# Attention's scores from three rounded products, expert weights split where they are used, a shorter choice of tokens

## The reference, cut to what matters

```python
h = ln(x) * g + b + shift(t)
q, k, v = split(h @ Wqkv.T)                 # 16 heads of 64
q, k = ln64(q), ln64(k)                     # per head, with scale and bias
o = softmax(q @ k.T / 8) @ v                # 256 x 256 scores per head and batch
x = x + o @ Wout.T
gate = softmax(x @ Wgate.T)                 # 8 experts
vals, idx = top_k(gate.T, 512)              # each expert takes its 512 best tokens
y = gelu(ln(x[idx]) @ fc1[e].T + b1) @ fc2[e].T + b2
x[idx] += y * vals
```

## Time and profile before

| | |
|---|---|
| median of three runs | 1504.6 us (1504.4 to 1504.73) |
| profiled execution, its own time | 1506.99 us |
| its span, first to last instruction | 1505.2 us |
| granted TensorE clock over the span | 0.98 |
| TensorE (PE) busy | 1411.1 us, 94% |
| ScalarE (ACT) busy | 974.7 us, 65% |
| VectorE (DVE) busy | 959.1 us, 64% |
| GpSimd (POOL) busy | 777.3 us, 52% |
| DMA | 138.79 MB, 92 GB/s |

### The profile page before, as it was taken

The page is one execution under the profiler, slowest core; times in us unless marked ns, Lnnn a source line. Parts: engine busy times, 40 slices in busy tenths (PEclk is TensorE's granted clock), DMA queues, the critical chain, the costliest instruction groups (busy, mean ns, idle before and its releaser), DMA issues. The chain is left out here.

```text
span 1505.2 us, 31379 instructions
## 1 busy us (share of the span) xinstructions
PE 1411.1 (94%) x9953; PEld 1164.0 (77%) x9953; DVE 959.1 (64%) x2244; ACT 974.7 (65%) x2601; POOL 777.3 (52%) x736
## 2 busy tenths in 40 slices
PE   4799999997999999999999999999999787999997
PEld 3799999985667777777777777777777566899996
DVE  5876666644576676676667667667756558565652
ACT  4556666545788788787787878878877640345452
POOL 3566667544455554654655554565555420264633
PEclk9899999998999999999999999999999999899998
DMA  5342222110122221221222221222222335267652
GB/s 154 91 135 68 65 68 70 47 36 21 50 71 78 85 79 64 91 84 64 76 84 82 79 84 63 77 91 85 69 66 78 101 107 229 83 194 228 196 168 28
DMA packets 92391, 138.79 MB, mean 92 GB/s; under 512 B 8656, under 2 KB 61824, under 8 KB 92160
## 3 DMA queue, kind: packets, MB, share of 16 engines
q1 hardware_dynamic: 84032, 126.30, 25.8%
q0 software_dynamic: 6144, 8.39, 2.9%
q10 hardware_dynamic: 2112, 2.88, 0.6%
HBM read 87.20 MB, written 50.35 MB: 91 GB/s over the span
## 5 line engine op out<-in xcount | busy, mean ns | idle before, releaser
L1301 POOL TENSOR_TENSOR prob<-prob,share_p 128x512 f32<-128x512 f32 x256 | 274.1, 1076 | 373.7 <-DVE share_p L1407 373.7
L1401 DVE TENSOR_REDUCE shift<-bank 128x2 f32<-128x512 f32 x256 | 164.8, 685 | 245.1 <-PE bank L1060 245.0
L1199 ACT ACTIVATE prob<-bank,shift 128x256 f32<-128x256 f32 x512 | 235.5, 473 | 99.6 <-DVE shift L1401 99.6
L147 PE MATMUL bank<-wqkv_h,rowsT_h 128*128 128x512 f32 x384 | 160.0, 417 | 5.7 <-PEq L313 3.5
L1086 PE MATMUL bank<-pT,v 128*64 128x256 f32 x1024 | 140.5, 396 | 16.4 <-ACT pT L1273 16.3
L147 PE MATMUL bank<-wqkv_l,rowsT_h 128*128 128x512 f32 x384 | 152.4, 397 | 0.0
L147 PE MATMUL bank<-wqkv_h,rowsT_l 128*128 128x512 f32 x384 | 152.4, 397 | 0.0
L1060 PE MATMUL bank<-landing 64*128 64x256 f32 x1024 | 145.4, 402 | 2.7 <-ACT prob L1199 2.7
L1073 PEld LDWEIGHTS bank<-ident,prob 128*128 128x128 f32 x1024 | 109.3, 141 | 43.9 <-issue 41.8
L1296 POOL TENSOR_TENSOR raw_qk<-raw_qk,rq 128x512 f32<-128x512 f32 x128 | 138.0, 1094 | 8.4 <-DVE rq L1355 8.4
L1073 PE MATMUL bank<-ident,prob 128*128 128x128 f32 x1024 | 140.5, 280 | 0.6 <-POOL prob L1301 0.4
(11 more groups left out here) (285 smaller groups left out, 4062.3 us busy)
## 6 DMA issues: line engine op xcount, KB each, us to landing
ew_raw<-in_fc1s SPq DMA_DIRECT2D x32, 256.0 KB, 3.2
split_w1h<-ew_h SPq DMA_DIRECT2D x32, 256.0 KB, 2.0
split_w1l<-ew_l SPq DMA_DIRECT2D x32, 256.0 KB, 2.5
ew_raw<-in_fc2s SPq DMA_DIRECT2D x32, 256.0 KB, 2.9
split_w2h<-ew_h SPq DMA_DIRECT2D x32, 256.0 KB, 2.1
split_w2l<-ew_l SPq DMA_DIRECT2D x32, 256.0 KB, 2.5
ew_h<-split_w1h SPq DMA_DIRECT2D x8, 1024.0 KB
ew_l<-split_w1l SPq DMA_DIRECT2D x8, 1024.0 KB
```

Source lines behind the costliest of these rows:

```text
L147: last = nc.tensor.matmul(out, a, b, start=(n == 0), stop=(n == 3 * len(ks) - 1))
L1199: last = nc.scalar.activation(prob[at][:, n, :], score_bank[side][:, n * T:(n + 1) * T], ACT.Exp, bias=shift[:, at, n:n + 1], scale=-1.0, ...
L1301: nc.gpsimd.tensor_tensor(prob[at][:, :, :], prob[at][:, :, :], share[:, at, :].unsqueeze(2).to_broadcast([P, TT, T]), ALU.mult).then_inc( ...
L1401: nc.vector.tensor_reduce(shift[:, s % 2 * 2 + side, :], score_bank[side][:, :].rearrange("p (n m) -> p n m", n=TT), AX, ALU.min).then_inc ...
```

## The change

Five things are changed together.

1. **Scores.** The normalised q and k, after transposing, scale and bias, go back to `raw`; ScalarE rounds each 128 x 512 block into `qT_h`/`kT_h` (pairs `HIGH_PAIR`) and GpSimd subtracts into `qT_l`/`kT_l` (`LOW_PLACE`). `scores` makes three fp32r products a side in place of one fp32 product. The first scores of a batch wait for six low parts, the fifth pair's for all eight.
2. **The order of a batch.** The `h` fill goes from slot 8 to 2, the second `proj` from slot 10 to 6, the q and k fills to slots 5 and 7 to 13; the value chunks from pairs 3 and 4 to 4 and 5; the normalising of q and k starts one slot earlier; GpSimd's residual sum goes from pair 6 to 5, and `a_l` and the low parts come behind both scalings of a pair.
3. **Expert weights.** Only experts 0 and 1 are split during attention, one piece a batch instead of four. For experts 2 to 7 the raw weights (2 MB an expert) are loaded in the experts' stage; ScalarE makes the high parts, VectorE the low parts of `fc1`'s weights, and GpSimd, behind its scatters, those of `fc2`'s.
4. **The choice of tokens.** The threshold is spread by one transpose, the masks are compared in place from the gates, and the counts go through fp32r products directly; the waits for the stores move from the end of attention into the choice's SyncE program.
5. **Records** are fp32 and not fp32r, and their 32 products go in turn to four column groups of the array.

```diff
-TR_FILLS = [("x2", 0, 1), ("gates", 0, 3), ("proj", 0, 4), ("qk", 0, 5), ("qk", 1, 6), ("qk", 2, 7), ("h", 0, 8), ("qk", 3, 9),
-            ("proj", 1, 10), ("qk", 4, 11), ("qk", 5, 12), ("qk", 6, 13), ("qk", 7, 14)]
+TR_FILLS = [("x2", 0, 1), ("h", 0, 2), ("gates", 0, 3), ("proj", 0, 4), ("qk", 0, 5), ("proj", 1, 6)] + [("qk", j, 6 + j) for j in range(1, 8)]
...
+QK_ORDER = [1, 0, 2, 3, 4, 6, 5, 7]
+HIGH_PAIR = [3, 4, 5, 5, 6, 6, 7, 7]
+LOW_PLACE = [(3,1),(4,1),(5,1),(5,1),(6,1),(6,1),(7,1),(7,1)]
...
-CHUNK_PAIRS = [6, 6, 7, 7, 0, 0, 1, 1, 3, 3, 4, 4]
+CHUNK_PAIRS = [6, 6, 7, 7, 0, 0, 1, 1, 4, 4, 5, 5]
...
-MEAN_SLOT, SEED_PAIR, NORM_SLOT = (1, 5), (1, 3), (4, 8)
+MEAN_SLOT, SEED_PAIR, NORM_SLOT = (1, 5), (1, 3), (3, 7)
...
-X2_PAIR = 6
+PIECE_PAIRS = 2, 3
+X2_PAIR = 5
...
+        raw = landing[:, 0:2, :].rearrange("p i (m n) -> p (i m) n", n=512)
...
+        qT_h, qT_l, kT_h, kT_l = (sbuf(s, n, [P, 12, T], F32R) for n in ("qT_h", "qT_l", "kT_h", "kT_l"))
+        v = [landing[:, 2 + i, :].rearrange("p (t n) -> p t n", t=TT) for i in range(2)]
...
+        o_h, o_l = (sbuf(s, f"o_{p}", [P, HW // P + 2, T], F32R) for p in "hl")
...
+        def block_of(parts, j, its):
+            e = QK_ORDER[j]
+            part = parts[e % QKC // 2]
+            at = 4 + 4 * its if e % 2 else 0
+            return part[:, at:at + 4, e // QKC * P:(e // QKC + 1) * P]
...
+                def store_piece(b, odd):
+                    wait(sp, ew_piece, 32, b, 32)
+                    for n, part in enumerate((ew_h, ew_l)):
+                        sp.dma_start(piece(halves[odd * 2 + n], b, odd), part[:, :].bitcast(F32)).then_inc(ew_stored, 16)
...
                     b = t + 3
                     if live(b):
                         wait(sp, tr_h, 1, b - 1, 1)
                         sp.dma_start(x1[:, :, :], x1_rows[bass.ds(b * T, T), :].rearrange("(t p) d -> p t d", p=P)).then_inc(x1_in, 16)
-                    pieces(t, (2,))
+                    if live(t):
+                        store_piece(t, odd)
+                    if live(t) and live(t + 1):
+                        load_piece(t + 1, 1 - odd)
...
-                sp.wait_ge(x2_stored, 16 * NB)
-                sp.wait_ge(x2n_stored, 16 * NB)
-                sp.wait_ge(ew_stored, 128 * NB)
...
                     if s == 0:
-                        wait(pe, out_qk, 8, t, 8)
+                        wait(pe, qk_lo, 8, t, 6)
+                    if s == 4:
+                        wait(pe, qk_lo, 8, t, 8)
                     wait(pe, exped, H, t, 2 * s)
+                    at = s if s < 4 else s + 4 * odd
                     for n in range(TT):
-                        for side in range(2):
-                            r = slice(side * HD, (side + 1) * HD)
-                            mm = nc.tensor.matmul(score_bank[side][:, n * T:(n + 1) * T], qT[odd][r, s, n * P:(n + 1) * P],
-                                                  kT[odd][r, s, :], start=True, stop=True)
-                            if n == TT - 1:
-                                mm.then_inc(scored, 1)
+                        for i, (q, k) in enumerate(((qT_h, kT_h), (qT_h, kT_l), (qT_l, kT_h))):
+                            for side in range(2):
+                                r = slice(side * HD, (side + 1) * HD)
+                                mm = nc.tensor.matmul(score_bank[side][:, n * T:(n + 1) * T], q[r, at, n * P:(n + 1) * P],
+                                                      k[r, at, :], start=(i == 0), stop=(i == 2))
+                                if n == TT - 1 and i == 2:
+                                    mm.then_inc(scored, 1)
...
                         wait(act, tr_qk, 8, b, j + 1)
-                        if isinstance(b, int) and b == 1:
-                            act.wait_ge(wo_lo, FIRST_LO + 1)
-                        dst, g = (qT, QN_G) if j % 4 < 2 else (kT, KN_G)
-                        nc.scalar.activation(dst[its][:, j % 2 * 4:j % 2 * 4 + 4, j // 4 * P:(j // 4 + 1) * P],
-                                             tr[:, :].rearrange("p (m n) -> p m n", m=4), ACT.Identity,
+                        g = QN_G if QK_ORDER[j] % QKC < 2 else KN_G
+                        nc.scalar.activation(raw_block(j), tr[:, :].rearrange("p (m n) -> p m n", m=4), ACT.Identity,
                                              bias=cols[:, g + 1:g + 2], scale=cols[:, g:g + 1]).then_inc(out_qk, 1)
...
-                        wait(act, tr_qk, 8, b - 1, e + 1)
+                        wait(act, qk_lo, 8, b - 1, QK_ORDER.index(e) + 1)
...
+                        for j in range(8):
+                            if live(t + 1) and HIGH_PAIR[j] == s:
+                                wait(act, out_qk, 8, t + 1, j + 1)
+                                nc.scalar.activation(block_of((qT_h, kT_h), j, 1 - odd), raw_block(j), ACT.Copy).then_inc(qk_hi, 1)
...
-                        if live(t) and s % 2 == 0:
-                            wait(act, ew_in, 64, t, 16 * (s // 2 + 1))
-                            wait(act, ew_stored, 128, t, 32 * (s // 2))
-                            nc.scalar.activation(ew_h[:, :], ew_raw[:, :], ACT.Copy).then_inc(ew_hi, 1)
+                        if live(t) and s == PIECE_PAIRS[0]:
+                            wait(act, ew_piece, 32, t, 16)
+                            wait(act, ew_stored, 32, t - 1, 32)
+                            nc.scalar.activation(ew_h[:, :], ew_raw[:, :], ACT.Copy).then_inc(ew_piece, 8)
...
+                def low_parts(b, odd, s, place):
+                    for j in range(8):
+                        if live(b) and LOW_PLACE[j] == (s, place):
+                            wait(pool, qk_hi, 8, b, j + 1)
+                            nc.gpsimd.tensor_tensor(block_of((qT_l, kT_l), j, 1 - odd), raw_block(j),
+                                                    block_of((qT_h, kT_h), j, 1 - odd).bitcast(F32), ALU.subtract).then_inc(qk_lo, 1)
...
@@ -1320,12 +1345,13 @@
                             nc.gpsimd.tensor_tensor(x2[:, :, :], proj[:, :, :], x2[:, :, :], ALU.add).then_inc(x2_done, 1)
                         if live(t):
                             divide(t, s, 0)
+                        if live(t):
+                            divide(t, s, 1)
                         if live(far) and not first(far) and s == SPLIT_PAIR:
                             wait(pool, a_hi, 1, far, 1)
                             wait(pool, chunk_done, 12, far - 1, 12)
                             nc.gpsimd.tensor_tensor(a_l[:, :, :], aT[:, :, :], a_h[:, :, :].bitcast(F32), ALU.subtract).then_inc(a_lo, 1)
-                        if live(t):
-                            divide(t, s, 1)
+                        low_parts(new, odd, s, 1)
...
+                        if live(t) and s == PIECE_PAIRS[1]:
+                            wait(dve, ew_piece, 32, t, 24)
+                            wait(dve, ew_stored, 32, t - 1, 32)
+                            nc.vector.tensor_tensor(ew_l[:, :], ew_raw[:, :], ew_h[:, :].bitcast(F32), ALU.subtract).then_inc(ew_piece, 8)
...
+                    for arrived, n in zip(stored, (16, 16, 32)):
+                        sp.wait_ge(arrived, n * NB)
+                    for e in range(EARLY):
+                        load_halves(sp, w1_in, (w1_h, w1_l), halves[0:2], e)
+                        load_halves(sp, w2_in, (w2_h, w2_l), halves[2:4], e)
+                    load_raw(sp, w1_raw, a["fc1s"], EARLY, 0, 0)
+                    load_raw(sp, w2_raw, a["fc2s"], EARLY, 0, 1)
...
+                    pe.wait_ge(found, 1)
+                    nc.tensor.transpose(banks[2][:, 0:P], prefix[:, 0:1].to_broadcast([P, P]), ident[:, :]).then_inc(spread_found, 1)
...
-                    nc.tensor.matmul(banks[6][:, 0:4], tables[:, 3 * P:4 * P], mask_count[:, :], start=True, stop=False)
...
+                    counts = [mask_count[:, q:q + 1].to_broadcast([P, P]) for q in range(4)]
+                    pair = lambda i: ahead[:, i:i + 2, :].rearrange("p i c -> p (i c)")
+                    for q, table in ((0, 1), (1, 1), (2, 0)):
+                        nc.tensor.matmul(banks[5][:, 0:2 * P], counts[q], pair(table), start=(q == 0), stop=False)
+                    nc.tensor.matmul(banks[5][:, P:2 * P], counts[3], ahead[:, 0, :], start=False, stop=False)
+                    nc.tensor.matmul(banks[4][:, 0:2 * P], counts[0], pair(0), start=True, stop=False)
+                    nc.tensor.matmul(banks[4][:, P:2 * P], counts[1], ahead[:, 0, :], start=False, stop=False)
                     for n, mask in ((1, tied_b), (0, above_b)):
-                        pe.wait_ge(masks_out, n + 1)
+                        pe.wait_ge(masks_out, 2 - n)
...
-                        link.note(vec.tensor_reduce(prefix[:, :], passed[:, :], AX, ALU.max))
+                        last = vec.tensor_reduce(prefix[:, :], passed[:, :], AX, ALU.max)
+                        if n == DIGITS - 1:
+                            last.then_inc(found, 1)
```

(32 more changed lines are left out.)

183 lines of the change are left out of this document (76 added, 107 removed).

## The result

The changed kernel takes 1523.0 us (median of 4 runs, 1520.0 to 1526.1) against 1504.7 before: ratio 1.0118, 95% interval 1.0100 to 1.0136. It is slower by 1.2%; the forecast was 1484.0 us, faster by 1.4%, in a range that ended at 1499. The profiled execution took 1521.5 us, its span 1519.7, 14.5 more than before.

What follows compares the result with a forecast made beforehand. TensorE was taken to bound attention and experts. Scores -19.2, seam +1.0, lead-in -2.0, attention's end -1.2, choice -1.9 and experts +2.7 sum to -20.6 us: 1504.6 to 1484.0 us, range 1469 to 1499.

Steps and rivals of the forecast that it cites:

- Scores: Attention's scores: six fp32r turns replace four fp32 ones, 0.15 us less a pair, -19.2 us over 128 pairs.
- the cover of 0.12 us: Pairs 5 and 6 of a batch: ScalarE finishes emptying the even fill 0.12 us before TensorE's odd fill needs it.
- The loop's seam: Attention's loop jump: ScalarE arrives about 0.2 us later relative to TensorE, in five turns, +1.0 us.
- Experts: Experts' stage: +0.4 us for each of six experts and +0.3 for the first record, +2.7 us (-2 to +14).
- Records: Experts' 64 small fp32 products: 1.3 us instead of 1.00, +0.3 us each (-0.3 to +1.8).
- low parts of `fc2`: GpSimd, behind an expert's scatters: ready within 0.2 us of TensorE's need, or up to 0.9 us late.
- Lead-in: Before the first scores: reordered fills against added GpSimd low parts, -2 us (-5 to +3).
- End of attention: Between last logits and the choice: the wait for the last store moves to SyncE, -1.2 us (0 to -1.4).
- choice: Choice of tokens: 1.1 us replaces 2.7 between counts and ranks, plus another small saving, -1.9 us (-1 to -2.3).
- Single file: Scores rival: fp32r products of different row halves do not overlap, +0.58 us a pair, 1577 us; chance 0.10.
- The experts pay: Experts rival: records in single file (+14 us) or low parts at 1.57 us, 1489 to 1496 us; chance 0.10.
- slower: Whole kernel slower by over 0.2%: chance 0.12, 0.10 from unoverlapped score products, 0.02 from ScalarE or GpSimd taking over.

Runs made afterwards that it cites:

- e9: Changed kernel with fc2 low parts on VectorE, plus four GpSimd subtractions nobody reads behind every expert's scatters, against the changed kernel: 1521.8 us.
- e11: Changed kernel with 45 instructions more in TensorE's stream near 20 us and fc2 low parts on VectorE, against the changed kernel: 1483.4 us.

## Why the prediction was wrong, by its steps

- **Scores, -19.2.** Right. Both sides run side by side: the 12 instructions start at 1016.28 and the transposes at 1017.19, 0.91 us as forecast, in turns of 0.12 behind a first one of 0.22:

```profile
1016.28 0.39 PE L1073 MATMUL bank<-kT_h,qT_h 64*128 64x256 f32 x2
1016.50 0.28 PE L1073 MATMUL bank<-kT_l,qT_h 64*128 64x256 f32 x2
1016.62 0.28 PE L1073 MATMUL bank<-kT_h,qT_l 64*128 64x256 f32 x2
...
1017.19 1.09 PE L1086 MATMUL bank<-ident,prob 128*128 128x128 f32 x8
```

- **ScalarE, GpSimd and the cover of 0.12 us in a batch.** Right: 44.91 and 38.89 us of 52.12 (forecast 45.3 and 40.0), no idle TensorE.
- **The loop's seam, +1.0. This step failed.** It read the 1.39 us of the earlier trace rows as ScalarE's lateness and added 0.2 to it, for five turns where the trace has four seams (four waits, 5.2 us in all). It did not count instructions: four more product instructions and their weight loads a pair take the loop's body on TensorE from 1572 to 1699 (the records between two jumps), and the four seams then cost 27.9 us more. The row "issue" at the jump and the instruction queue were in the trace of before, and said that ScalarE's code was already brought anew in each turn. The insertion of 45 instructions shows the cause, the longer body of the kernel before shows that the new scores have no part in it but their number.
- **Experts, +2.7. This step failed too.** Records: 0.3 was to be lost on each, and 0.18 is won (their 64 instructions take 0.82 us until the next group starts; 1.00 before). The low parts of `fc2` by GpSimd cost 2.4 to 2.9 us an expert and 18.0 us in all, not 0.4 an expert. The forecast saw that GpSimd had 0.2 us to spare and took its scatters and subtractions as they were in the earlier trace rows; they came later (last scatter 20.2 us behind the start of the second product group, for 18.0) and ran to 1388.6. And it costed VectorE at nothing, because it had room. Room is not the question: GpSimd's subtractions, even unread, stop VectorE's for 5 us (e9), and TensorE with it.
- **Lead-in, -2 (-5 to +3).** -4.1; the walk pair by pair had said -4. **End of attention -1.2, choice -1.9:** from the last logits to the choice 1.2 us less (0.86 for 2.03); the choice itself 1.5 less, where 1.9 was forecast.
- **The rivals.** Single file did not happen. "The experts pay" named the right engine, at 0.9 us an expert and not 2.4 to 2.9, and for its lateness alone. No rival held the seam; the case "slower" was carried by the wrong mechanism.

With both failed steps mended and nothing else (e11) the time is 1483.4 us for a forecast of 1484.0. That this is so close is in part luck. The span of its profiled execution is 24.4 us under before, for 20.6 forecast (its ratio, 0.9847, would make 1481.6 us beside the 1504.6 of before), and by stage it is: lead-in -4.7 (forecast -2.0), attention -15.9 (-19.4, with the seams and the end), choice -2.0 (-1.9), experts -1.9 (+2.7). The seams of that run are still 2.1 to 3.7 us above a steady batch, where before it was 1.4, and the lead-in and the records, both costed too high, make up for it.

Why the insertion of 115 met one slow jump in four, and the one of 150 one quick jump in four, stays open; both bodies end just inside their eighth block. The effect of GpSimd on VectorE was seen for subtractions, products, a scaling and a copy beside runs of four subtractions, and was not tried for other operations of GpSimd.

## What to carry to other kernels

Before adding instructions to a loop's body, count them per engine and look in the DMA view for instruction packets inside the loop: an engine that has none keeps its loop, and a few more instructions, or the same ones at another place, can end that at several microseconds a turn (8.4 here). A stop named "issue" inside a group, or right behind a jump, was a fetch here and no semaphore. And before moving an elementwise operation to an idle GpSimd, look at what VectorE does at that time, not at how busy it is.
